# Cross attention on one core: turning the scores' rows in two row tiles, with a weighing put in front and every engine's order written anew

## The chip, the cores and the metric

One core of one Trainium2 chip runs the whole program. The metric is device time in microseconds; of several runs of a kernel the median is taken. The engines are TensorE (PE: matmuls and transposes, with its weight loads), VectorE (DVE), ScalarE (ACT), GpSimd (POOL) and SyncE (SP), whose queue issues the transfers.

## The reference

```python
x = x + tanh(g_xattn[0]) * cross(ctx, ctx, layernorm(x), mask, wq, bq, wk, bk, wv, bv, wo, bo)
x = x + tanh(g_ffn[0]) * switch(layernorm(x), Wq, Wk, Wv, Ws, Wd, Wo)

def cross(v, k, q, ...):                                  # x: (32, 112, 256), ctx: (32, 375, 256), 16 heads of 16
    qh, kh, vh = split(q @ wq + bq), split(k @ wk + bk), split(v @ wv + bv)
    logits = einsum('bhqd,bhkd->bhqk', qh, kh) / sqrt(16) + mask * -1e9
    attn = softmax(logits)
    return merge(einsum('bhqk,bhkd->bhqd', attn, vh)) @ wo + bo
```

The second layer (`switch`) is an attention over the 112 rows of x whose values and outputs are mixed from 8 experts chosen by a top 2 of gates. All is float32.

## The kernel before

The program has a short preparation, then a first half (`cross`, the first layer, all 32 batches) and a second half (`switch`, the second layer). The change is in `cross` alone.

**Groups and heads.** A batch has 16 heads in NG = 4 groups of G = 4. For each head PE computes the scores (`scores`, L439): 112 rows of queries by 375 keys, from three-part bfloat16 stacks (`Q_stack`, `K_stack`), into one of two banks. DVE adds the mask, copies the scores to `raw` and takes the row maximum (`score_max`, L759). POOL subtracts, giving `shifted` (`shift`, L876). When the four heads of a group are shifted, PE turns them (`turn`, L448): each head's 112 x 384 is turned in KC = 3 pieces of 128 keys, so 12 transposes a group, into the three banks of `bank_t`, one bank for each k. ACT takes the exponentials, one instruction a bank, into `probsT` (`exps`, L665). PE multiplies them with the values, weighing (`weigh`, L462): one matmul with 32 columns of weights for each k and head, into `bank_o` (the trace records 24 a group: each float32 one twice).

**Around them.** After the four groups ACT copies `headsT`, PE turns it back (`heads_back`, L470), DVE divides by the sums (`normalise`), PE turns (`heads_turn`, L477) and projects (`project`, L483), and DVE adds the result to x (`residual`). In the body of batch b PE also works ahead: for b + 2 the transposes of the context (`transposes`, L398), the keys in two halves (`keys`, L406), the turned x (`turn_x`, L414) and the queries (`queries`, L422), and for b + 1 the values (`values`, L430). Keys and queries are split into bfloat16 parts: keys by ACT, POOL (`key_rest`, L884) and DVE (`key_third`), queries by ACT (`query_copy`) and DVE (`split_queries`). They are stored to HBM and read back in stacked form (`exchange`, on SP's queue: L336, L338, L339, L344, L348).

**Order.** There is no scheduler. Every engine has a `body(b, ...)` that lists its work for one batch by hand, and runs it in that order; `batches` calls it for all 32, with the first two and the last two apart. Semaphores tie the engines: `turned`, `exp_done`, `pv_done`, `shift_done`, `scores_read` and so on, each counted through the batches. `shifted` and `probsT` have two buffers by the group's parity, `bank_t` one, so the turning of a group waits for the exponentials of the one before it, bank by bank. PE's order in a body of before is:

scores 0, 1; turning 3 of b - 1; score 2; transposes; score 3; weighing 3 of b - 1; score 4; keys 0; score 5; turning 0; scores 6, 7; keys 1; weighing 0; heads_back; score 8; turning 1; score 9; heads_turn; score 10; values 0, 1; score 11; weighing 1; score 12; project; score 13; turning 2; turn_x; scores 14, 15; values 2; queries; weighing 2.

The second half turns its scores in the manner that the change brings to the first: `HALVES` of 64 and 48 rows (L1169), then exponentials of ACT that write each half's columns (L1312).

Of the kernel before, what the change touches and what calls it, by code (L numbers as in the profile page):

```python
# [256 lines left out]
def cross(nc, z, d, c):  # L257
# [3 lines left out]
    VW = 32  # L261
    o = c.o
    with ExitStack() as ctx:
# [15 lines left out]
        probsT = sb("probsT", [KP, 2, KC, G * S])  # L279
# [32 lines left out]
        turned, exp_done, pv_done = sem("turned"), sem("exp_done"), sem("pv_done")  # L312
        headsT_copied, heads_ready, recip_done, heads_done = sem("headsT_copied"), sem("heads_ready"), sem("recip_done"), sem("heads_done")
# [73 lines left out]
        def _(pe):  # L387
# [123 lines left out]
            def body(b, p, i, first, ahead, last):  # L511
# [3 lines left out]
                S_ = lambda *hs: [scores(b, p, i, h, first) for h in hs]  # L515
                S_(0, 1)
                if back:
                    turn(b - 1, NG - 1, False)
                S_(2)
                if ahead:  # L520
                    transposes(b + 2, i + 1, p)
                S_(3)
                if back:
                    weigh(b - 1, 1 - p, NG - 1, False)
                S_(4)
                if ahead:
                    keys(b + 2, p, 0)
                S_(5)
                turn(b, 0, first)
                S_(6, 7)  # L530
                if ahead:
                    keys(b + 2, p, 1)
                weigh(b, p, 0, first)
# [7 lines left out]
                turn(b, 1, False)  # L541
                S_(9)
# [4 lines left out]
                S_(10)  # L547
                if front:
                    values(1 - p, 0)
                    values(1 - p, 1).then_inc(va_ready, 1)  # L550
                S_(11)
                weigh(b, p, 1, False)
                S_(12)
                if back:
                    project(b - 1)
                S_(13)
                turn(b, 2, False)
# [5 lines left out]
                S_(14, 15)  # L563
# [4 lines left out]
                if ahead:  # L568
                    queries(b + 2)
                elif front:  # L570
                    open_gates(b + 2 - B)
                weigh(b, p, 2, False)
# [37 lines left out]
            batches(pe, body)  # L610
            open_proj(0)
# [9 lines left out]
        def _(act):  # L621
# [57 lines left out]
            def body(b, p, i, first, ahead, last):  # L679
                second = isinstance(b, int) and b == 1  # L680
                if not first:
# [8 lines left out]
                if ahead:  # L690
# [7 lines left out]
                if ahead:  # L698
                    copy_x(b + 2)
                    query_copy(b + 2, p, i + 1)  # L700
                else:
                    e = b + 2 - B
                    act.wait_ge(o.xt_ready, e + 1)
                    act.activation(o.xnT[:, :, e, :], bank_ab[:, 0, 0:EC * S].rearrange("p (e s) -> p e s", e=EC), ACT.Copy).then_inc(o.xt_copied, 1)
                    if e == 0:
                        act.wait_ge(o.gates_ready, 1)
                        act.activation(o.gates[:, :, :].rearrange("s g e -> s (g e)"), bank_ab[0:S, 0, 0:2 * z.H2 * z.X], ACT.Copy).then_inc(o.gates_copied, 1)
# [35 lines left out]
        def _(dve):  # L743
# [65 lines left out]
            def body(b, p, i, first, ahead, last):  # L809
                second = isinstance(b, int) and b == 1  # L810
                if ahead:
# [3 lines left out]
                score_max(b, first, 0, 1)  # L815
                if not first and not last:
                    split_queries(b + 1)
                score_max(b, first, *range(2, 7))
# [7 lines left out]
                score_max(b, first, 8, 9, 10)  # L826
                if not last:
                    value_copy(b + 1, 1 - p, 0)
                score_max(b, first, 11, 12)
                if ahead:  # L830
                    key_third(b + 2, p)
                if not first:
                    residual(b - 1)
                score_max(b, first, 13, 14, 15)
                if not last:
                    value_copy(b + 1, 1 - p, 1)

# [31 lines left out]
        def _(pool):  # L869
            def shift(b, g, first):  # L870
# [693 lines left out]
```

## Time and profile before

| | us |
|---|---|
| median of 3 runs | 1300.96 |
| lowest and highest | 1298.34, 1303.64 |
| the profiled execution's own time | 1308.71 |
| its span, first to last instruction | 1307.0 |

The profile is of one execution. Its first half ends near 669 us of the span. A timeline row gives the start in us from the span's start, how long the merged instructions lasted from the first's start to the last's end, engine, line, operation, what it writes and reads, and how many there are. Pieces of PE overlap a little, since matmuls are pipelined.

### The profile page before, as it was taken

To read this page: it belongs to the slowest core of one execution; us is meant where nothing else is said; L and a number is where in the kernel's file an instruction comes from. 1 tells how busy PE (TensorE), PEld (TensorE's weight loads), DVE (VectorE), ACT (ScalarE), POOL (GpSimd) and SP (SyncE) were. 2 spreads that over 40 slices of the span, in tenths; PEclk is the share of its full clock that TensorE was granted. 3 is DMA by queue.
4 is the path that set the end of the run, shared out by engine and by line. 5 is a ranking of instruction groups with operands and counts; after the bars stand their busy time and mean duration, and the time that the engine had idled before them with its cause. 6 is when DMAs were issued, how large, how long until landed. Compare 5 with 4: busy or idle time off the path is not lost. (4 is left out here: it accounts for less than half of the span.)

```text
span 1307.0 us, 40360 instructions
## 1 busy us (share of the span) xinstructions
PE 1246.8 (95%) x15928; PEld 1017.5 (78%) x15928; DVE 866.8 (66%) x2455; ACT 611.9 (47%) x1353; POOL 550.3 (42%) x823
## 2 busy tenths in 40 slices
PE   5799999999999999999988999999999999999986
PEld 4577777787777777777667888888888888888874
DVE  2566766766766766766666667767766776676651
ACT  3455556556556556556434444334343443434331
POOL 3476676676676676666621122122122212221111
PEclk9999999999999999999999999999999999999997
DMA  8898897797787787786415666656666665666662
GB/s 224 192 196 190 191 199 170 165 189 159 161 184 159 158 185 157 161 185 146 103 43 116 151 137 137 155 133 141 142 149 131 139 161 132 141 143 150 144 133 77
DMA packets 262975, 200.21 MB, mean 153 GB/s; under 512 B 195906, under 2 KB 243844, under 8 KB 258692
## 3 DMA queue, kind: packets, MB, share of 16 engines
q1 hardware_dynamic: 262788, 197.64, 68.3%
q8 instruction: 127, 2.08, 0.7%
q14 instruction: 60, 0.49, 0.2%
HBM read 125.49 MB, written 72.11 MB: 151 GB/s over the span
## 5 line engine op out<-in xcount | busy, mean ns | idle before, releaser
L876 POOL TENSOR_SCALAR shifted<-raw,neg_max 112x375 f32<-112x375 f32 x512 | 304.5, 603 | 195.9 <-DVE neg_max L759 131.2
L759 DVE CUSTOM_DVE_ANT_0 raw<-bank_s,maskb 112x375 f32<-112x375 f32 x512 | 269.2, 545 | 119.5 <-issue 78.0
L665 ACT ACTIVATE probsT<-bank_t 128x448 f32<-128x448 f32 x384 | 181.0, 547 | 162.8 <-PE bank_t L448 162.8
L448 PE MATMUL bank_t<-ident,shifted 112*128 112x112 f32 x1536 | 170.3, 261 | 3.4 <-POOL shifted L876 3.4
L448 PEld LDWEIGHTS bank_t<-ident,shifted 112*128 112x128 f32 x1536 | 156.0, 141 | 22.3 <-POOL shifted L876 19.0
L439 PE MATMUL bank_s<-K_stack,Q_stack 128*112 128x375 bf16 x512 | 158.2, 337 | 13.5 <-DVE neg_max L759 8.1
L1467 POOL TENSOR_TENSOR mix_bd<-pm_te,tok 128x448 f32<-128x448 f32 x32 | 30.8, 963 | 232.8 <-DMA pm_te<-pm_dram 232.8
L1394 DVE TENSOR_REDUCE max<-bank_s 112x4 f32<-112x448 f32 x128 | 78.7, 615 | 74.8 <-PE bank_s L1157 74.8
L1109 PE MATMUL bank_ab<-xnT,wq2T 128*128 128x224 f32 x512 | 109.5, 357 | 0.8 <-ACT qT L1287 0.6
L1109 PE MATMUL bank_ab<-xnT,wk2T 128*128 128x224 f32 x512 | 109.7, 357 | 0.0
L1109 PEld LDWEIGHTS bank_ab<-xnT,wq2T 128*128 128x128 f32 x512 | 94.3, 190 | 11.6 <-issue 7.4
L1109 PEld LDWEIGHTS bank_ab<-xnT,wk2T 128*128 128x128 f32 x512 | 94.2, 190 | 10.2 <-issue 7.4
L462 PE MATMUL bank_o<-probsT,V 128*32 128x112 f32 x3072 | 101.2, 263 | 0.1
L462 PEld LDWEIGHTS bank_o<-probsT,V 128*32 128x32 f32 x3072 | 69.1, 109 | 39.4 <-issue 27.8
L439 PEld LDWEIGHTS bank_s<-K_stack,Q_stack 128*112 128x112 bf16 x512 | 62.7, 130 | 45.1 <-DVE neg_max L759 22.7
L203 POOL TENSOR_SCALAR var_eps<-moments 112x1 f32<-112x1 f32 x32 | 7.1, 223 | 213.5 <-DVE moments L199 213.4
L406 PE MATMUL bank_ab<-ctxT,wk_sb 128*128 128x375 f32 x256 | 93.1, 488 | 1.2 <-ACT ctxT L626 1.2
L430 PE MATMUL bank_ab<-wv_sb,ctxT 128*128 128x256 f32 x372 | 90.4, 379 | 0.0
L1397 DVE TENSOR_TENSOR shifted<-bank_s,max 112x448 f32<-112x448 f32 x128 | 79.9, 625 | 4.4
L430 PEld LDWEIGHTS bank_ab<-wv_sb,ctxT 128*128 128x128 f32 x372 | 68.8, 190 | 6.5
L1181 PEld LDWEIGHTS bank_g<-v,probsT 112*64 112x64 f32 (+1 forms) x1792 | 57.1, 130 | 19.7 <-issue 19.7
L1409 DVE COPY uT<-bank_g 128x448 f32<-128x448 f32 x32 | 20.0, 624 | 77.7 <-PE bank_g L1191 77.7
(144 smaller groups left out, 2250.7 us busy)
## 6 DMA issues: line engine op xcount, KB each, us to landing
K_stack<-k_dram SPq DMA_DIRECT2D x64, 562.5 KB, 7.5
k_dram<-k_parts SPq DMA_DIRECT2D x32, 562.5 KB, 5.1
att_dram<-att_q SPq DMA_DIRECT2D x32, 511.0 KB, 4.3
att_th<-att_dram SPq DMA_DIRECT2D x32, 511.0 KB, 5.3
v_dram<-mv SPq DMA_DIRECT2D x32, 455.0 KB, 7.2
v<-v_dram SPq DMA_DIRECT2D x32, 455.0 KB, 4.0
K_stack<-k_dram SPq DMA_DIRECT2D x32, 375.0 KB, 9.4
Q_stack<-q_dram SPq DMA_DIRECT2D x64, 168.0 KB, 9.2
```

The lines of the kernel that those rows point to most:

```text
L406: last = nc.tensor.matmul(bank_ab[:, t, 0:S2], c.wk[:, e, t * P:(t + 1) * P], ctxT[:, p, e, 0:S2], start=(e == 0), stop=(e == EC - 1))
L430: last = nc.tensor.matmul(dst, ctxT[:, p, e, k * KP:(k + 1) * KP], c.wv[:, e, :], start=(e == 0), stop=(e == EC - 1))
L439: nc.tensor.matmul(bank_s[h % 2][0:S, 0:S2], Q_stack[:, p, h, :], K_stack[:, p, h, :], start=True, stop=True).then_inc(scores_ready, 1)
L448: last = nc.tensor.transpose(bank_t[0:KP, k, j * S:(j + 1) * S], shifted[:, g % 2, j, k * KP:(k + 1) * KP], c.ident[0:S, 0:S])
L462: last = nc.tensor.matmul(bank_o[j * VW:(j + 1) * VW, g * S:(g + 1) * S], V[:, p, k, G * g + j, :], probsT[:, g % 2, k, j * S:(j + 1) * S] ...
L665: act.activation(probsT[:, g % 2, k, :], bank_t[0:KP, k, 0:G * S], ACT.Exp).then_inc(exp_done, 1)
L759: dve.tensor_tensor_reduce(raw[:, g % 2, j, :], bank_s[h % 2][0:S, 0:S2], c.maskb[:, :], -1.0, -LEAST, ALU.add, ALU.min, neg_max[:, g % 2, ...
L876: pool.tensor_scalar(shifted[:, g % 2, j, 0:S2], raw[:, g % 2, j, :], -1.0, neg_max[:, g % 2, j:j + 1], ALU.mult, ALU.add).then_inc(shift_ ...
L1109: last = nc.tensor.matmul(bank_ab[:, 0, m * 2 * S:(m + 1) * 2 * S], w, xnT[:, e, 2 * h:2 * h + 2, :].rearrange("p r s -> p (r s)"), start= ...
L1181: last = nc.tensor.matmul(weighed(half, m)[lo:hi, :], probsT[:, half, m, lo:hi], v[:, p, 2 * G * half + m, :], start=True, stop=True)
L1394: dve.tensor_reduce(neg_max[:, g % 2, :], sc, AXX, ALU.max).then_inc(max_done, 1)
L1397: dve.tensor_tensor(shifted[:, g % 2, :, :], sc, neg_max[:, g % 2, :].unsqueeze(2).to_broadcast([S, G, S]), ALU.subtract).then_inc(shift_d ...
```

## The change

`turn` splits the 112 rows of queries into `HALVES` of 64 and 48. A unit is one k and one head, u = 4k + j, twelve in a group. Each unit is turned by two transposes, one with rows 0 to 63 and one with rows 64 to 111 of the array. The lower half's units 0 to 7 go to bank 0 and the upper half's units 0 to 9 to bank 1; the rest share bank 2. The upper half runs with units 10 and 11 first, and the lower half's unit 8 waits for `upper_done`, so that both halves never write bank 2 at a time. `turned` is counted once a group instead of once a bank. `exps` has four instructions a group, one for each entry of `PLACES` (512, 480, 256 and 96 columns), which write the half's columns of each unit, and counts four. `turn` waits for all exponentials of the group before, and `weigh` for all of its own. `probsT` is indexed by unit.

PE's order becomes: transposes; scores 0, 1; weighing 2 of b - 1; turning 3 of b - 1; scores 2, 3; keys 0; score 4; weighing 3 of b - 1; scores 5, 6; keys 1; score 7; heads_back; score 8; turning 0; heads_turn; score 9; values 0, 1; score 10; weighing 0; turning 1; score 11; turn_x; score 12; project; score 13; queries; values 2; scores 14, 15; turning 2; weighing 1. ACT's, DVE's and POOL's orders follow. SP's queue is not touched.

```diff
+    UNITS, LOW = KC * G, z.S - 48
+    PLACES = ((0, 8, 0, 0, 0), (0, 10, 1, 1, 0), (8, 12, 0, 2, 0), (10, 12, 1, 2, 4 * LOW))
+    HALVES = ((0, LOW), (LOW, z.S))
...
-        probsT = sb("probsT", [KP, 2, KC, G * S])
+        probsT = sb("probsT", [KP, 2, UNITS, S])
...
             def turn(b, g, first):
                 pe.wait_ge(shift_done, H * b + G * g + G)
-                for k in range(KC):
-                    if not (first and g == 0):
-                        pe.wait_ge(exp_done, KC * (NG * b + g - 1) + k + 1)
-                    for j in range(G):
-                        last = nc.tensor.transpose(bank_t[0:KP, k, j * S:(j + 1) * S],
-                                                   shifted[:, g % 2, j, k * KP:(k + 1) * KP], c.ident[0:S, 0:S])
-                    last.then_inc(turned, 1)
+                if not (first and g == 0):
+                    pe.wait_ge(exp_done, len(PLACES) * (NG * b + g))
+
+                def one(half, u):
+                    lo, hi = HALVES[half]
+                    (bank, column), = [(bank, column + (u - first_u) * (hi - lo)) for first_u, end, h, bank, column in PLACES
+                                       if h == half and first_u <= u < end]
+                    k, j = u // G, u % G
+                    return nc.tensor.transpose(bank_t[0:KP, bank, column:column + hi - lo], shifted[lo:hi, g % 2, j, k * KP:(k + 1) * KP], c.ident[lo:hi, lo:hi])
+
+                for u in range(UNITS):
+                    if u == 8:
+                        pe.wait_ge(upper_done, NG * b + g + 1)
+                    one(0, u)
+                    last = one(1, (u + UNITS - 2) % UNITS)
+                    if u == 1:
+                        last.then_inc(upper_done, 1)
+                last.then_inc(turned, 1)
 
             def weigh(b, p, g, first):
...
+                pe.wait_ge(exp_done, len(PLACES) * (NG * b + g + 1))
                 for k in range(KC):
-                    pe.wait_ge(exp_done, KC * (NG * b + g) + k + 1)
                     for j in range(G):
                         last = nc.tensor.matmul(bank_o[j * VW:(j + 1) * VW, g * S:(g + 1) * S], V[:, p, k, G * g + j, :],
-                                                probsT[:, g % 2, k, j * S:(j + 1) * S], start=(k == 0), stop=(k == KC - 1))
+                                                probsT[:, g % 2, G * k + j, :], start=(k == 0), stop=(k == KC - 1))
...
             batches(pe, body)
+            weigh(B - 1, 1, NG - 2, False)
             open_proj(0)
             turn(B - 1, NG - 1, False)
             weigh(B - 1, 1, NG - 1, False)
...
             def exps(b, g, first):
                 if not (first and g < 2):
                     act.wait_ge(pv_done, NG * b + g - 1)
-                for k in range(KC):
-                    act.wait_ge(turned, KC * (NG * b + g) + k + 1)
-                    act.activation(probsT[:, g % 2, k, :], bank_t[0:KP, k, 0:G * S], ACT.Exp).then_inc(exp_done, 1)
+                act.wait_ge(turned, NG * b + g + 1)
+                for first_u, end, half, bank, column in PLACES:
+                    lo, hi = HALVES[half]
+                    act.activation(probsT[:, g % 2, first_u:end, lo:hi], bank_t[0:KP, bank, column:column + (end - first_u) * (hi - lo)].rearrange("p (u q) -> p u q", q=hi - lo),
+                                   ACT.Exp).then_inc(exp_done, 1)
...
             def body(b, p, i, first, ahead, last):
                 second = isinstance(b, int) and b == 1
+                if ahead:
+                    ctx_copy(b + 2, p, False)
                 if not first:
                     exps(b - 1, NG - 1, False)
                 if ahead:
-                    ctx_copy(b + 2, p, False)
+                    key_copy(b + 2, p, i + 1, 0)
                 if not first:
                     heads_copy(b - 1, second)
                 if ahead:
-                    key_copy(b + 2, p, i + 1, 0)
+                    key_copy(b + 2, p, i + 1, 1)
                 exps(b, 0, first)
-                if ahead:
-                    key_copy(b + 2, p, i + 1, 1)
-                exps(b, 1, first)
                 if not first:
                     out_copy(b - 1, second)
+                e = b + 2 - B
                 if ahead:
                     key_second(b + 2, p)
-                exps(b, 2, False)
-                if ahead:
                     copy_x(b + 2)
-                    query_copy(b + 2, p, i + 1)
                 else:
...
+                exps(b, 1, first)
+                if ahead:
+                    query_copy(b + 2, p, i + 1)
...
+                exps(b, 2, False)
```

On DVE `split_queries(b + 1)` moves to the front of the body, `moments_of` from the front to behind maximum 2, the first `value_copy` from behind maximum 10 to behind 9, `residual` stands behind maximum 12, `key_third` moves from behind maximum 12 to behind 13, and the second `value_copy` from the end to behind `key_third`. On POOL `key_rest` moves from behind shift 7 to before it.

## Rows read from the trace of the kernel before

**Rows 1.** The page, busy time by engine: us, share of the span, instructions.
```profile
PE 1246.8 (95%) x15928; PEld 1017.5 (78%) x15928; DVE 866.8 (66%) x2455; ACT 611.9 (47%) x1353; POOL 550.3 (42%) x823
```
**Rows 2.** Windows: us, busy time of each engine, PE's clock, DMA share, GB/s.
```profile
69.00:200.00 131.00, 129.73 (x1397) 104.30 (x1395) 91.78 (x306) 74.74 (x162) 88.88 (x134) 1.00 0.89 194
...
340.00:640.00 300.00, 294.25 (x3168) 235.09 (x3167) 208.72 (x693) 168.90 (x365) 202.30 (x308) 1.00 0.77 167
...
415.50:430.40 14.90, 14.90 (x143) 11.81 (x145) 10.09 (x35) 7.49 (x17) 11.58 (x18) 1.00 0.99 218
```
**Rows 3.** Who waited for whom, 69 to 625 us: us in total, times, longest.
```profile
PE bank_s L439 <- DVE neg_max L759: 6.3, 28, 0.6
```
**Rows 4.** Timeline of PE, 400 to 421 us.
```profile
400.84 0.65 PE L470 MATMUL bank_ab<-ident,headsT 128*112 128x128 f32 x4
...
401.49 1.32 PE L448 MATMUL bank_t<-ident,shifted 112*128 112x112 f32 x12
402.64 0.33 PE L439 MATMUL bank_s<-K_stack,Q_stack 128*112 128x375 bf16 x1
...
404.88 0.32 PE L439 MATMUL bank_s<-K_stack,Q_stack 128*112 128x375 bf16 x1
405.13 0.78 PE L462 MATMUL bank_o<-probsT,V 128*32 128x112 f32 x24
405.85 0.37 PE L439 MATMUL bank_s<-K_stack,Q_stack 128*112 128x375 bf16 x1
...
411.51 0.53 PE L439 MATMUL bank_s<-K_stack,Q_stack 128*112 128x375 bf16 x2
...
414.10 0.78 PE L462 MATMUL bank_o<-probsT,V 128*32 128x112 f32 x24
415.09 0.37 PE L439 MATMUL bank_s<-K_stack,Q_stack 128*112 128x375 bf16 x1 [0.21 <-DVE neg_max L759]
...
420.26 0.65 PE L470 MATMUL bank_ab<-ident,headsT 128*112 128x128 f32 x4
```
**Rows 5.** Timeline of the second half, 1004.6 to 1005.6 us.
```profile
1004.65 0.66 PE L1169 MATMUL bank_t<-ident,shifted 64*112 64x64 f32 x16
...
1005.13 0.71 PE L1157 MATMUL bank_s<-kT,qT 64*112 64x112 f32 x10
1005.35 0.60 ACT L1312 ACTIVATE probsT<-bank_t 112x512 f32<-112x512 f32 x1
```
**Rows 6.** Groups by line, 340 to 640 us: busy us, mean ns of one.
```profile
L759 DVE CUSTOM_DVE_ANT_0 raw<-bank_s,maskb 112x375 f32<-112x375 f32 x247 | 129.9, 545 | 53.7 <-issue 37.4 <-PE bank_s L439 14.2
L665 ACT ACTIVATE probsT<-bank_t 128x448 f32<-128x448 f32 x186 | 87.7, 547 | 77.4 <-PE bank_t L448 77.4
L884 POOL TENSOR_TENSOR k<-k,k_parts 128x750 f32<-128x750 f32 x15 | 23.5, 1563 | 4.7 <-ACT k_parts L636 4.6
L677 ACT ACTIVATE outT<-bank_ab 128x224 f32<-128x224 f32 x16 | 6.0, 378 | 0.0
```
**Rows 7.** Timeline of SP's queue, 411 to 432 us.
```profile
414.60 0.38 SPq L338 DMA_DIRECT2D q_dram<-q_parts  x1
...
415.67 1.40 SPq L344 DMA_DIRECT2D K_stack<-k_dram  x3
417.68 1.37 SPq L348 DMA_DIRECT2D Q_stack<-q_dram  x3
```
**Rows 8.** DMA issues, 340 to 640 us, last row 69 to 200 us: median us to landing.
```profile
k_dram<-k_parts SPq DMA_DIRECT2D x15, 562.5 KB, 5.0
...
Q_stack<-q_dram SPq DMA_DIRECT2D x16, 112.0 KB, 9.9
...
k_dram<-k_parts SPq DMA_DIRECT2D x7, 562.5 KB, 6.8
```
**Rows 9.** Timeline of the last group, 655 to 690 us.
```profile
661.35 1.32 PE L448 MATMUL bank_t<-ident,shifted 112*128 112x112 f32 x12
...
661.99 1.42 ACT L665 ACTIVATE probsT<-bank_t 128x448 f32<-128x448 f32 x3 [2.62 <-PE bank_t L448]
```

More of the change, by code:

```diff
@@ L312, in cross @@
         turned, exp_done, pv_done = sem("turned"), sem("exp_done"), sem("pv_done")
+        upper_done = sem("upper_done")
         headsT_copied, heads_ready, recip_done, heads_done = sem("headsT_copied"), sem("heads_ready"), sem("recip_done"), sem("heads_done")
@@ L515, in body @@
                 S_ = lambda *hs: [scores(b, p, i, h, first) for h in hs]
+                if ahead:
+                    transposes(b + 2, i + 1, p)
                 S_(0, 1)
                 if back:
+                    weigh(b - 1, 1 - p, NG - 2, False)
                     turn(b - 1, NG - 1, False)
-                S_(2)
+                S_(2, 3)
                 if ahead:
-                    transposes(b + 2, i + 1, p)
-                S_(3)
+                    keys(b + 2, p, 0)
+                S_(4)
                 if back:
                     weigh(b - 1, 1 - p, NG - 1, False)
-                S_(4)
-                if ahead:
[L527 to L530, printed above, removed]
+                S_(5, 6)
                 if ahead:
                     keys(b + 2, p, 1)
-                weigh(b, p, 0, first)
+                S_(7)
                 if last:
@@ L540, in body @@
                 S_(8)
-                turn(b, 1, False)
-                S_(9)
+                turn(b, 0, first)
                 if ahead:
@@ L546, in body @@
                     heads_turn(b - 1)
-                S_(10)
+                S_(9)
                 if front:
@@ L550, in body @@
                     values(1 - p, 1).then_inc(va_ready, 1)
+                S_(10)
+                weigh(b, p, 0, first)
+                turn(b, 1, False)
                 S_(11)
[L552 to L557, printed above, removed]
                 if ahead:
@@ L562, in body @@
                     open_x(b + 2 - B)
-                S_(14, 15)
+                S_(12)
+                if back:
+                    project(b - 1)
+                S_(13)
+                if ahead:
+                    queries(b + 2)
+                elif front:
+                    open_gates(b + 2 - B)
                 if front:
@@ L567, in body @@
                     values(1 - p, 2).then_inc(vb_ready, 1)
-                if ahead:
[L569 to L572, printed above, removed]
+                S_(14, 15)
+                turn(b, 2, False)
+                weigh(b, p, 1, False)
             def turn_weights(*numbers):
@@ L680, in body @@
                 second = isinstance(b, int) and b == 1
+                if ahead:
+                    ctx_copy(b + 2, p, False)
                 if not first:
@@ L810, in body @@
                 second = isinstance(b, int) and b == 1
+                if not first and not last:
+                    split_queries(b + 1)
+                score_max(b, first, 0, 1, 2)
                 if ahead:
@@ L814, in body @@
                     o.moments_of(dve, c.X[0:S, b + 2 - B, :], b + 2 - B)
[L815 to L818, printed above, removed]
+                score_max(b, first, 3, 4, 5, 6)
                 if ahead:
@@ L825, in body @@
                     normalise(b - 1, second)
-                score_max(b, first, 8, 9, 10)
+                score_max(b, first, 8, 9)
                 if not last:
                     value_copy(b + 1, 1 - p, 0)
-                score_max(b, first, 11, 12)
+                score_max(b, first, 10, 11, 12)
+                if not first:
+                    residual(b - 1)
+                score_max(b, first, 13)
                 if ahead:
                     key_third(b + 2, p)
-                if not first:
-                    residual(b - 1)
-                score_max(b, first, 13, 14, 15)
                 if not last:
                     value_copy(b + 1, 1 - p, 1)
+                score_max(b, first, 14, 15)
             def copy_weights(*numbers):
@@ L869, in _, with shift @@
         def _(pool):
-            def shift(b, g, first):
-                for j in range(G):
+            def shift(b, g, first, members=range(G)):
+                for j in members:
                     h = G * g + j
-                    free = [] if j or (first and g < 2) else [(turned, KC * (NG * b + g - 1))]
+                    free = [] if j or (first and g < 2) else [(turned, NG * b + g - 1)]
                     wait_all(pool, v_set, (scores_read, H * b + h + 1), *free)
@@ L903, in body @@
                     o.inverse_deviation(pool, b + 2 - B)
-                shift(b, 1, first)
+                shift(b, 1, first, range(G - 1))
                 if ahead:
                     key_rest(b + 2, p)
+                shift(b, 1, first, (G - 1,))
                 shift(b, 2, first)
```

10 lines of the change are left out of this document (4 added, 6 removed).

## The prediction

> **What bounds the kernel now.** First the busy shares [rows 1]: TensorE (PE) is busy 95% of the span. The shares mix two halves, so the windows come next [rows 2]: in 340 to 640 us, the middle of the first half, PE is busy 294.25 of 300 us at clock 1.00, VectorE (DVE) 208.72, ScalarE (ACT) 168.90, GpSimd (POOL) 202.30, DMA 0.77. DMA stands at 0.89 before 200 us, where x is still being loaded. Then who waited for whom, 69 to 625 us [rows 3]: PE's longest wait, scores for the row maximum, is 6.3 us in all. So the first half is PE's instruction stream, and the last view is that stream [rows 4]: the same piece (L470) starts at 400.84 and 420.26, a batch of 19.42 us, and I find one stall in it, where the score at 415.09 follows a weighing that began at 414.10 and elsewhere hands over after 0.71 to 0.72 (405.13 to 405.85): 0.28 us.
>
> The reader is to see how PE pieces hand over. A piece is drawn until its last result is out. The next begins 0.16 to 0.17 us before that end when it uses the array in the same shape (401.49+1.32=402.81, next at 402.64), but only 0.07 us before it when the shape changes: the score at 404.88 ends at 405.20, the weighing (128 rows by 32 columns) begins at 405.13. A change therefore costs about 0.09 us, and a score is followed after 0.16 us by a turning but after 0.25 us by a weighing [rows 4].
>
> **The turning in two row tiles.** Before, a group's turning is 12 whole transposes, 1.15 us from its start to the next piece's (401.49 to 402.64), 0.096 us each [rows 4]. No row has the split one with 128 columns, but the second half turns 64 and 48 rows with 112 columns [rows 5]: from the start of 16 halves to the next piece, of the same shape, are 0.48 us. If the first pair takes 0.10, as a whole one does, the other seven take 0.055 each. Drawn, the 16 halves last 0.66 us; twelve pairs will be 0.66+4x0.055 = 0.88 us, and as the next piece has another shape it begins 0.07 before that end: 0.81 us. The bounds for the wider weights: nothing more, or all in proportion, 0.055x128/112 = 0.063 us a pair, which is +0.10 us a group. I take nothing, since with whole transposes 0.096 us holds a load of 128 columns too and did not wait for it longer than for 112 moving ones; the other end is kept. The wait inside the turning, before unit 8, is for a matmul started six pairs, 0.33 us, earlier whose result is out 0.66-0.48+0.04 = 0.22 later: nothing, at worst 0.05.
> Sum: 4x(1.15-0.81) = -1.36 us a batch.
> The Trainium skill, TensorEngine Tiling (Array Packing), section Instruction Overhead, gives each matmul some 60 cycles beside its columns, so that narrow ones save little. By it at 2.4 GHz (the granted 1.00) a whole transpose is (112+60)/2.4 = 72 ns and a half of 64 columns 52 ns, an estimate of 20 ns saved a unit where the rows give 41: over 48 units and 29 batches 29 us less than my sum, some 1293. The rows have 96 ns for the whole one, so the trace does not agree with it there.
>
> **Changes of shape.** Before: four weighings a batch entered at +0.09 (their way out is in the 0.71). After: turnings 0 and 2 follow a score or ordinary piece, +0.18; turnings 1 and 3 stand right behind a weighing, whose way out is paid anyway, 0; the weighing of group 1 follows turning 2, whose way out is in the 0.81, so one entry less, -0.09. Net +0.09. Without "another group in front" this would be +0.36.
>
> **Order on PE.** The same pieces otherwise. More scores now stand before another score or the keys (0.20 us: two drawn as 0.53, one as 0.33) than before a transpose (0.16): +0.07 over the order. The stall of 0.28 goes if score 4 no longer follows score 2 so closely: weighing and keys lie between. PE's sum: 19.42-1.36+0.09+0.07-0.28 = 17.94 us.
>
> **Do the others keep up at 17.94?** I wrote the new orders as a timetable from the rows' durations, t in us from score 0. PE's steps are read from the 31 pieces between 400.84 and 420.26, of which [rows 4] has the first and last: keys 1.26, values 1.72 and 0.86, project 0.86, queries 0.97, heads_back 0.49, transposes 0.65, heads_turn and turn_x 0.19, weighing 0.71. Then scores 0, 1 start at 0 and 0.20; weighing 2 0.46; turning 3 1.17; scores 2, 3 1.98, 2.19; keys 2.39; score 4 3.65; weighing 3 3.90; scores 5, 6 4.61, 4.82; keys 5.02; score 7 6.28; heads_back 6.44; score 8 6.93; turning 0 7.18; heads_turn 8.00; score 9 8.20; values 8.36; score 10 10.08; weighing 0 10.33; turning 1 11.05; score 11 11.86; turn_x 12.02; score 12 12.21; project 12.42; score 13 13.28; queries 13.48; values 14.45; scores 14, 15 15.32, 15.52; turning 2 15.78; weighing 1 16.59; transposes 17.30; the next score 0 17.95.
>  Per batch ACT has 11 us of work, DVE 13.5, POOL 13.1 (shares of [rows 2] by 19.42), ACT's to grow by 0.2: no engine becomes the bound. ACT: exps are now four of 512, 480, 256 and 96 columns. A 512 one with this very output pattern takes 0.60 [rows 5]; 448 take 0.547 and 224 take 0.378 [rows 6], so 0.57, 0.40 and 0.28 for the rest. Three of 0.547 are drawn as 1.42 [rows 9], so each starts 0.12 before the end of the one ahead: 1.48 us for all four. None can begin until the whole turning is out, 0.10 behind it, say ([rows 5] has 0.04, 1005.31 to 1005.35): they end 0.88+0.10+1.48 = 2.46 after it began, where before they ended 663.41-661.35 = 2.06 after. The rest of ACT's queue behind them (keys, headsT) has idle time. What is late next:
>
> turning 2 at 15.8 ends 16.7, exps end 18.2, weighing 2 stands at 17.94+0.46 = 18.4: slack 0.1;
> turning 3 at 1.2, exps end 3.6, weighing 3 at 3.9: slack 0.2;
> turning 0 at 7.2, exps 9.6, weighing 0 at 10.3: 0.6; group 1 over 2.
> score 6 at 4.8 needs maximum 4 (score 4 at 3.65, read 0.46 later, 0.55 on DVE [rows 6]): slack 0.1; heads_turn behind turning 0 at 8.0 needs heads from 7.5: none.
> POOL: the key rest (1.56 us [rows 6]) is put before shift 7; that shift ends 9.7 and turning 1 waits for it at 11.0. Turnings come later than before against the scores, but shifts of group 2 need only turning 0 (8.0; shift 8 at 9.7).
> I charge 0.1 us a batch for these tight places.
> Costed at nothing: the split of queries put first on DVE (the queries are copied by 15.6, so the split ends 0.6, maximum 0 by 1.0, and its bank is wanted at 1.98), x's moments, add of bias, and the moved values: each has a gap of over 0.3 us behind it in that timetable.
>
> **DMA.** Before, the transfers of a batch run as one burst: busy 0.99 from 415.5 to 430.4, idle in the 4 us before [rows 2]. It starts when the queries are split (first q_dram issue 414.60, 3.1 us after score 0 at 411.51), K_stack 415.67, the last Q_stack issue 418.6 plus 9.9 to land = 428.5 [rows 7, 8], 2.4 us before the next score 0 (411.51+19.42 = 430.9). After, the split is ready at 0.6 instead of 3.1, but the keys' store (issued 15.5, 5.0 to land) must have landed too: 20.5-17.94 = 2.6 into the batch. K_stack then goes at 2.6 and all is in by 2.6+12.8 = 15.4 to 16: 2 us of slack, as before. In the batches that also load x, DMA is busy 0.89x19.42 = 17.3 of the new 17.94 us [rows 2], and the store takes 6.8 rather than 5.0 us [rows 8]: K_stack at 4.4, in by 17.2, with no room for a longer burst. I charge 0.5 us a batch over six: 3 us; the bounds are 0 and 1 us each.
>
> **Sum.** Batches 1 to 29 have the full order: 29x(1.48-0.1) = 40.0; early DMA +3. Batch 0 lacks turning 3 and saves perhaps 0.7; batches 30 and 31 hold no keys and wait for the maxima anyway: 0. At the end nothing hides the exps, so the last group's 2.46 against 2.06 us [rows 9] is +0.4, and weighing 2, which now stands 1.52 after the start of turning 2 (0.81+0.71), waits for its exps about 1.0. Total -40.0+3-0.7+1.4 = -36.3 us. The profiled execution took 1308.71 us (span 1307.0) and would take 1272.4; the runs' median, 1300.96, is 7.75 lower, and I carry that difference over: 1264.7, say **1265 us**.
>
> **Rivals.**
> The chain through the exps binds in part (weighings 2 and 3 at slack 0.1 and 0.2, DVE's maximum likewise). Each 0.1 us more of wait in two groups is 0.2x29 = 6 us. With 0.2 to 0.5 us more a group, or pairs at 0.063 us as well (4x0.10x29 = 12 us), 1273 to 1290. For it: slacks are thin. Against: the same way of writing out the old order gives 19.44 for the 19.42 measured.
> The halves take turns in the array instead of running side by side: a pair then costs 0.055+0.042 = 0.097 us, 4x11x0.042 = 1.85 us a batch more than I take, which eats 1.48: +0.37x29 = 11 us, **1312**. It decides from 0.089 us a pair on. Against: 16 halves in 0.66 us [rows 5].
> The split saves half as much, a pair at 0.076 us, halfway between 0.055 and the 0.097 above: 4x11x0.021x29 = 27 us of the gain go, **1291**. For it: a 128-column load in a row tile is in no row. Against: the same loads fit in 0.096 us with 112 moving columns. The Trainium skill's fixed cost per matmul, cited above, would come out near this.
> Nothing comes of it: the bound moves to DMA and the burst follows period for period. That wants over 19.3 us of transfers a batch; the rows show 15 (17.3 early). Time 1298 to 1304.
> Also possible: no tight place binds and early DMA hides: 3+3 us less, 1259.
>
> **How the numbers follow.** The measurement can tell 0.5%, 6.5 us. My forecast, 1256 to 1273, the 1259 in it: 0.62. Partly bound, 1273 to 1290: 0.22. Half the saving, about 1291: 0.03. Below 1256: 0.04. No change: 0.04. Slower: 0.05, 0.03 of it the halves taking turns, 0.02 the exps' chain longer by over 0.8 us a group. The range goes from 1254 (3 us of scatter of the runs below 1257, the bare 1.48 in 29 batches) to 1283, the middle of the partly bound case: some 0.2 lie outside. Faster 0.91, same 0.04, slower 0.05.
>
> **What would show it.** In the profile after: a group's 24 half transposes drawn as 0.88 us; the piece behind at +0.81; scores of one place 17.95 to 18.1 apart from 200 to 600 us; four exps of 0.60, 0.57, 0.40, 0.28. Wrong would be: weighings waiting for ACT over 0.2 us, K_stack landing behind score 0, a pair above 0.063 us, PE's clock under 1.00 in the first half, or a period that stays over 18.6.

## The result and the profile after

Medians of four runs each on one chip: 1300.49 us before, 1264.70 us after (1261.05 to 1267.14). The ratio is 0.972, with an interval of 0.9696 to 0.9743. The forecast was 1265 us. The profiled execution took 1262.39 us, its span is 1260.7.

The windows of the kernel after, as in [rows 2]: us, busy time of each engine (PE, PE's loads, DVE, ACT, POOL), clock, DMA share, GB/s.
```profile
69.00:200.00 131.00, 130.89 (x1821) 100.71 (x1820) 100.06 (x328) 82.18 (x204) 96.64 (x147) 1.00 0.94 203
340.00:600.00 260.00, 257.75 (x3623) 197.69 (x3624) 197.16 (x646) 159.85 (x395) 189.63 (x289) 1.00 0.81 178
```
PE is still the bound: 257.75 of 260 us, at clock 1.00. The transfers are denser, 0.81 for 0.77, and 0.94 for 0.89 where x is loaded.

PE's timeline of one batch after, the answer to [rows 4]:
```profile
405.11 0.96 PE L460 MATMUL bank_t<-ident,shifted 64*128 64x64 f32 x24
406.00 0.78 PE L482 MATMUL bank_o<-probsT,V 128*32 128x112 f32 x24
406.71 0.87 PE L406 MATMUL bank_ab<-ident,ctx_in 128*128 128x128 f32 x6
407.42 0.48 PE L447 MATMUL bank_s<-K_stack,Q_stack 128*112 128x375 bf16 x2
407.84 0.78 PE L482 MATMUL bank_o<-probsT,V 128*32 128x112 f32 x24
408.55 0.95 PE L460 MATMUL bank_t<-ident,shifted 64*128 64x64 f32 x24
409.44 0.53 PE L447 MATMUL bank_s<-K_stack,Q_stack 128*112 128x375 bf16 x2
...
414.50 0.96 PE L460 MATMUL bank_t<-ident,shifted 64*128 64x64 f32 x24
415.46 0.38 PE L497 MATMUL bank_ab<-ident,heads 112*128 112x112 f32 x2
...
418.54 0.95 PE L460 MATMUL bank_t<-ident,shifted 64*128 64x64 f32 x24
419.42 0.37 PE L447 MATMUL bank_s<-K_stack,Q_stack 128*112 128x375 bf16 x1
...
423.17 0.96 PE L460 MATMUL bank_t<-ident,shifted 64*128 64x64 f32 x24
```
Turning 2 starts at 405.11 and again at 423.17: a batch of 18.06 us for 19.42 [rows 4]. A turning is drawn as 0.95 to 0.96 us and hands over after 0.89 (408.55 to 409.44), where it was 1.15. Only at 415.46 does the next piece start when the turning is out, not 0.07 us before: heads_turn waits for the heads, which DVE finishes at 415.31.

ACT's timeline of the same batch after, and the exps by size (the groups of 340 to 600 us), for [rows 6]:
```profile
406.18 1.48 ACT L686 ACTIVATE probsT<-bank_t 128x512 f32<-128x512 f32 x4 [1.13 <-PE bank_t L460]
...
409.61 1.48 ACT L686 ACTIVATE probsT<-bank_t 128x512 f32<-128x512 f32 x4 [1.18 <-PE bank_t L460]
```
```profile
L686 ACT ACTIVATE probsT<-bank_t 128x512 f32<-128x512 f32 x57 | 34.0, 596 | 45.2 <-PE bank_t L460 45.2
L686 ACT ACTIVATE probsT<-bank_t 128x480 f32<-128x480 f32 x57 | 32.4, 569 | 0.0
L686 ACT ACTIVATE probsT<-bank_t 128x256 f32<-128x256 f32 x57 | 22.5, 395 | 0.0
```
The exps begin 0.11 us behind the turning's end (405.11+0.96 = 406.07) and last 1.48 us. Those of group 2 are done at 407.66, and weighing 2 starts at 407.84: 0.18 us to spare.

SP's queue after, for [rows 7], and landings in 340 to 600 us, for [rows 8]:
```profile
404.86 0.38 SPq L344 DMA_DIRECT2D k_dram<-k_parts  x1
407.83 0.38 SPq L346 DMA_DIRECT2D q_dram<-q_parts  x1
...
409.67 1.38 SPq L352 DMA_DIRECT2D K_stack<-k_dram  x3
```
```profile
k_dram<-k_parts SPq DMA_DIRECT2D x14, 562.5 KB, 4.4
...
Q_stack<-q_dram SPq DMA_DIRECT2D x15, 112.0 KB, 10.0
```
The queries' store goes 0.4 us after score 0 (407.42) instead of 3.1, K_stack 2.25 us after it. Over the batches of the full order the stacks land 2.2 to 4.7 us before they are wanted.

The end of the first half after, for [rows 9]:
```profile
622.71 0.78 PE L482 MATMUL bank_o<-probsT,V 128*32 128x112 f32 x24 [0.93 <-ACT probsT L686]
623.42 1.97 PE L528 MATMUL bank_s<-wv2T,xnT 128*112 128x512 f32 x4
625.32 0.96 PE L460 MATMUL bank_t<-ident,shifted 64*128 64x64 f32 x24
628.21 0.78 PE L482 MATMUL bank_o<-probsT,V 128*32 128x112 f32 x24 [1.93 <-ACT probsT L686]
```
Weighing 2 waits 0.93 us for its exps and weighing 3 waits 1.93.

Where the time went, by the two traces: from the first score of batch 0 to that of batch 31, 602.2 us before and 560.8 after, -41.4; from there to the second half's first queries 25.7 and 29.7, +4.1. Together -37.3 us. Two pieces changed sides of these cuts. The transposes of batch 2 now stand before the first score, where they take 1.3 us (43.73 to 45.04), and weighing 2 of batch 30 stands behind the first score of batch 31 (0.7 us). Like for like the batches gave -39.4 us, the end +3.3, and the change -36.0.

The start took 2.4 us more (the first score at 45.0 for 42.6), 1.3 of it these transposes. The second half, whose code is the same, took 625.0 for 636.5 us. Of these 11.5 us, 7.6 lie in its last 60 us or so. There the granted clock stood at half (1.2 GHz) for 23.9 us before and for 10.3 us after; the same eight matmuls (`wo2T`, `uT`) last 3.6 to 3.7 us at that level and 1.95 at the full one. Another 2.8 us lie in its first 45 us; whether the first half's new end has a part in them is not shown. In the twelve other profiles of this study it takes 627 to 637 us, so the 625.0 is a short one. The profiled executions differ by 46 us and the medians by 36.

### The profile page after: what moved, and what is told of

It is laid out like the page before. It is cut to its first block and busy times, and to the rows that moved or that the text cites. A ratio compares the mean times of both kernels' runs of the same rounds, so it can differ in the third digit from the quotient of the medians.

```text
span 1260.7 us, 43560 instructions
## 1 busy us (share of the span) xinstructions
PE 1208.4 (96%) x17464; PEld 967.8 (77%) x17464; DVE 869.2 (69%) x2455; ACT 619.6 (49%) x1481; POOL 550.5 (44%) x823
## 5 line engine op out<-in xcount | busy, mean ns | idle before, releaser
L899 POOL TENSOR_SCALAR shifted<-raw,neg_max 112x375 f32<-112x375 f32 x512 | 326.0, 645 | 164.4 <-DVE neg_max L781 120.6
L781 DVE CUSTOM_DVE_ANT_0 raw<-bank_s,maskb 112x375 f32<-112x375 f32 x512 | 266.5, 544 | 102.8 <-issue 87.7
L686 ACT ACTIVATE probsT<-bank_t 128x512 f32<-128x512 f32 (+3 forms) x512 | 189.2, 459 | 104.2 <-PE bank_t L460 104.2
L447 PE MATMUL bank_s<-K_stack,Q_stack 128*112 128x375 bf16 x512 | 151.2, 336 | 4.9 <-DVE neg_max L781 4.6
L460 PEld LDWEIGHTS bank_t<-ident,shifted 64*128 64x128 f32 (+1 forms) x3072 | 105.3, 139 | 27.8 <-issue 24.5
L460 PE MATMUL bank_t<-ident,shifted 48*128 48x48 f32 (+1 forms) x3072 | 122.6, 226 | 0.0
L1133 PEld LDWEIGHTS bank_ab<-xnT,wk2T 128*128 128x128 f32 x512 | 94.1, 190 | 10.3 <-issue 7.4
L1311 ACT ACTIVATE qT<-bank_ab 128x448 f32<-128x448 f32 x64 | 34.8, 543 | 72.9 <-PE bank_ab L1133 72.9
```

The costliest lines, as they stand in the source:

```text
L447: nc.tensor.matmul(bank_s[h % 2][0:S, 0:S2], Q_stack[:, p, h, :], K_stack[:, p, h, :], start=True, stop=True).then_inc(scores_ready, 1)
L460: return nc.tensor.transpose(bank_t[0:KP, bank, column:column + hi - lo], shifted[lo:hi, g % 2, j, k * KP:(k + 1) * KP], c.ident[lo:hi, lo ...
L686: act.activation(probsT[:, g % 2, first_u:end, lo:hi], bank_t[0:KP, bank, column:column + (end - first_u) * (hi - lo)].rearrange("p (u q) ...
L781: dve.tensor_tensor_reduce(raw[:, g % 2, j, :], bank_s[h % 2][0:S, 0:S2], c.maskb[:, :], -1.0, -LEAST, ALU.add, ALU.min, neg_max[:, g % 2, ...
L899: pool.tensor_scalar(shifted[:, g % 2, j, 0:S2], raw[:, g % 2, j, :], -1.0, neg_max[:, g % 2, j:j + 1], ALU.mult, ALU.add).then_inc(shift_ ...
L1133: last = nc.tensor.matmul(bank_ab[:, 0, m * 2 * S:(m + 1) * 2 * S], w, xnT[:, e, 2 * h:2 * h + 2, :].rearrange("p r s -> p (r s)"), start= ...
```

## The experiments

A batch's time below is the median distance of two first scores, from each run's trace.

**Order alone, tiles alone.** `order_only` is the kernel before with the bodies of all engines as after (and weighing 2 in front of the end); `tiles_only` is the kernel after with the bodies of before. Short diffs against before and after:
```diff
 # order_only, against before
+                if ahead:
+                    transposes(b + 2, i + 1, p)
                 S_(0, 1)
                 if back:
+                    weigh(b - 1, 1 - p, NG - 2, False)
                     turn(b - 1, NG - 1, False)
...
 # tiles_only, against after
-                if ahead:
-                    transposes(b + 2, i + 1, p)
                 S_(0, 1)
-                if back:
-                    weigh(b - 1, 1 - p, NG - 2, False)
-                    turn(b - 1, NG - 1, False)
-                S_(2, 3)
+                if back:
+                    turn(b - 1, NG - 1, False)
+                S_(2)
+                if ahead:
+                    transposes(b + 2, i + 1, p)
+                S_(3)
...
```


> The new orders of all engines with the whole transposes and the three exps a group of before. Theory (PE's steps add up): a batch of 18.07 us plus 4 x 0.264 for whole turnings (1.151 for 0.887), less 0.18 for the entries of turnings 0 and 2, plus 0.09 for weighing 1 behind turning 2: 19.04 us, 0.37 under before, so some 1290 us. Rival (the order is what pays, by taking away waits): under 18.5 us a batch, 1275 or less. Rival (the order alone is worth nothing): 19.4 us, 1300.

> The turning in two row tiles and the four exps, in the orders of before. Theory: 19.42 - 1.06 + 4 x 0.09 for four entries into the row tiles = 18.72 us of PE's own work, and weighing 3 comes 1.96 us after the start of turning 3 but its exps end 2.5 after: a wait of 0.5 us, which may swallow the 0.28 of score 4. 19.0 to 19.3 us a batch, 1288 to 1297. Rival (exps are covered in the old order too): 18.7 to 18.8, 1281.

Measured: `order_only` 1286.02 us, ratio 0.9882 (0.9849 to 0.9916), 18.95 us a batch. `tiles_only` 1318.85 us, ratio 1.0126 (1.0102 to 1.0149), 19.71 us a batch. The first is 0.09 us under the sum of PE's steps (19.04); 0.28 us of its gain of 0.47 is the stall of score 4, whose weighing hands over after 0.71 there. The second is slower than before and beyond my expectation (19.0 to 19.3 us). PE's timeline of `tiles_only`:
```profile
414.08 1.03 PE L438 MATMUL bank_ab<-wv_sb,ctxT 128*128 128x256 f32 x4
415.13 1.15 PE L430 MATMUL bank_ab<-xnT,wq_sb 128*128 128x112 f32 x8
416.20 0.78 PE L482 MATMUL bank_o<-probsT,V 128*32 128x112 f32 x24
416.92 0.53 PE L447 MATMUL bank_s<-K_stack,Q_stack 128*112 128x375 bf16 x2
417.37 0.95 PE L460 MATMUL bank_t<-ident,shifted 64*128 64x64 f32 x24
...
419.12 0.32 PE L447 MATMUL bank_s<-K_stack,Q_stack 128*112 128x375 bf16 x1
419.97 0.78 PE L482 MATMUL bank_o<-probsT,V 128*32 128x112 f32 x24 [0.53 <-ACT probsT L686]
```
Weighing 3 (419.97) stands 0.85 us behind a score that hands over in 0.25: 0.60 us for the exps, as expected (0.5). What I had left out is, first, at 415.13: the values before the queries hand over after 1.05 us, and the queries take 1.07 to the next piece, where both were 0.86 and 0.97. On ACT the copy of the turned x stood behind four exps that now begin after the whole turning.

**One instruction moved in `tiles_only`.**
```diff
-                exps(b, 2, False)
                 if ahead:
                     copy_x(b + 2)
+                exps(b, 2, False)
+                if ahead:
                     query_copy(b + 2, p, i + 1)
```


> As tiles_only (19.71 us a batch), but ACT copies the turned x before the exps of group 2. Theory (the four exps hold up what stands behind them on ACT, which PE's queries wait for, 0.19+0.10 us a batch): the queries no longer wait, weighing 2 is late enough for the later exps: 19.42 us a batch, some 1310 us. The wait of weighing 3 for its exps stays at 0.6 us. Rival (only the wait at weighing 3 and the shapes cost): 19.7.

Measured: 1312.90 us, ratio 1.0045 (1.0023 to 1.0067), 19.42 us a batch. In its timeline the queries follow the values after 0.86 us again, and weighing 3 still waits:
```profile
408.76 0.82 PE L447 MATMUL bank_s<-K_stack,Q_stack 128*112 128x375 bf16 x2
409.42 1.03 PE L438 MATMUL bank_ab<-wv_sb,ctxT 128*128 128x256 f32 x4
410.28 1.04 PE L430 MATMUL bank_ab<-xnT,wq_sb 128*128 128x112 f32 x8
...
415.02 0.78 PE L482 MATMUL bank_o<-probsT,V 128*32 128x112 f32 x24 [0.52 <-ACT probsT L686]
```
The two scores of 408.76 also hand over late: score 14 after 0.46 us for 0.24 in the kernel before, as the weights of score 15 wait for DVE's maximum of score 13. So the old order's balance can be written out, by the same batch in both traces. The four turnings are 1.10 us shorter. Going into them and coming out of them costs 0.51 us (0.33 on the way in, 0.18 on the way out; I had set 0.36 in all). Weighing 3 waits 0.60, less the stall of 0.28 that is gone. Score 15 costs 0.22 and weighing 0, which waits for its exps, 0.08. That is 1.13 us against 1.10, and `tiles_only` loses 0.29 more at the queries.

**Changes of shape.** `apart` puts a score between a weighing and the turning next to it, in three places:
```diff
-                weigh(b, p, 0, first)
-                turn(b, 1, False)
-                S_(11)
+                weigh(b, p, 0, first)
+                S_(11)
+                turn(b, 1, False)
...
-                S_(14, 15)
-                turn(b, 2, False)
+                S_(14)
+                turn(b, 2, False)
+                S_(15)
                 weigh(b, p, 1, False)
```
and likewise score 1 between weighing 2 and turning 3.

> The kernel after, with one score moved between weighing 2 and turning 3, between weighing 0 and turning 1, and between turning 2 and weighing 1. Theory: three changes of shape more at 0.09 us each, less up to 0.04 for each score that no longer stands beside another: 0.15 to 0.27 us a batch more, 1269 to 1273. Rival (a change of shape costs nothing when an engine order around it is free): 18.07 us, 1265.

Measured: 1280.63 us, ratio 0.9827 (0.9793 to 0.9862), 18.49 us a batch, +0.42 for the three. More than the 0.15 to 0.27 expected. Its timeline:
```profile
414.78 0.32 PE L447 MATMUL bank_s<-K_stack,Q_stack 128*112 128x375 bf16 x1
415.04 0.96 PE L460 MATMUL bank_t<-ident,shifted 64*128 64x64 f32 x24
415.92 0.37 PE L447 MATMUL bank_s<-K_stack,Q_stack 128*112 128x375 bf16 x1
416.22 0.78 PE L482 MATMUL bank_o<-probsT,V 128*32 128x112 f32 x24
```
A score behind a piece of its own shape hands over to another shape after 0.26 us (414.78 to 415.04). One that is itself the first after a change lasts 0.37 for 0.32 and hands over after 0.30 (415.92 to 416.22). Against the 0.16 of a score amid its own shape a lone score between two changes costs 0.14 us, and three make the 0.42.

**Does the chain through the exps bind?** `five_exps`:
```diff
-    PLACES = ((0, 8, 0, 0, 0), (0, 10, 1, 1, 0),
+    PLACES = ((0, 4, 0, 0, 0), (4, 8, 0, 0, 4 * LOW), (0, 10, 1, 1, 0),
```


> The kernel after, with the exp of 512 columns as two of 256: the chain from turning to weighing is 0.16 us longer in every group. Theory (PE bound, slack of 0.18 and 0.22 us at weighings 2 and 3): 18.07 to 18.12 us a batch, 1265 to 1267. Rival (the chain through the exps binds): 0.16 us in two to four groups, 18.4 to 18.7, 1274 to 1283.

Measured: 1267.45 us, ratio 0.9734 (0.9709 to 0.9759), 18.07 us a batch. But the chain is not 0.16 us longer:
```profile
405.89 1.54 ACT L686 ACTIVATE probsT<-bank_t 128x256 f32<-128x256 f32 x5 [1.14 <-PE bank_t L460]
```
The five exps are drawn as 1.54 us for the 1.48 of four, since the second 256 columns start 0.28 us behind the first. The slack falls from 0.18 to 0.12 us at weighing 2 and from 0.22 to 0.16 at weighing 3. The chain does not bind, in this kernel or in the kernel after, but only 0.06 us more of it was put to the test; that 0.16 us would be covered is not shown.

**What spaces the pairs.** The turning came out at 0.89 us for the 0.81 of the sum. In the trace the two halves of a pair start within 20 ns of each other, so it is the pairs that are spaced. `load96`, `load124` and `load120` load and turn fewer of the 128 columns from batch 1 on (the rest of each piece is left out and keeps old values):
```diff
+                    wide = KP if b == 0 else 96
-                    return nc.tensor.transpose(bank_t[0:KP, bank, column:column + hi - lo], shifted[lo:hi, g % 2, j, k * KP:(k + 1) * KP], c.ident[lo:hi, lo:hi])
+                    return nc.tensor.transpose(bank_t[0:wide, bank, column:column + hi - lo], shifted[lo:hi, g % 2, j, k * KP:k * KP + wide], c.ident[lo:hi, lo:hi])
```


> The kernel after, but from batch 1 on each half transpose loads and turns 96 of the 128 columns; the last 32 of each piece are left out and keep older values. Theory (the weight load sets the spacing): a pair every 0.049 us, (96 columns by the line through 0.055 at 112 and 0.062 at 128), 4 x 11 x 0.013 = 0.6 us a batch less. Rival (the moving side has a floor, and 0.055 was it): a pair every 0.055 us, 0.3 us a batch less. Rival (neither, the wider piece was spaced by the rows of the group): 0.062.

> As load96 with 120 columns, the last 8 left out. Theory (load of 0.0623 x 120/128 = 0.058 above the floor of 0.055): a pair every 0.058 us, whatever the rule on multiples up to 8. Rival (multiples of 16): 0.10 or more.

> As load96 with 124 of 128 columns loaded and turned from batch 1 on, the last 4 left out. moved125 had a pair of half transposes every 0.109 us with 125 columns, load96 every 0.055 with 96. Theory (an odd number of columns is what makes a load slow): a pair every 0.060 us, between 0.055 and 0.062. Rival (only multiples of 16 are fast): 0.105 to 0.109.

The weight loads of the turning by width, one row of each kernel, 340 to 600 us (mean ns of one stands before the second bar). `load96`:
```profile
L461 PEld LDWEIGHTS bank_t<-ident,shifted 64*96 64x96 f32 x696 | 42.2, 123 | 12.3 <-issue 11.0 <-POOL shifted L900 1.3
```
`load120`:
```profile
L461 PEld LDWEIGHTS bank_t<-ident,shifted 64*120 64x120 f32 x696 | 44.6, 134 | 12.3 <-issue 11.0 <-POOL shifted L900 1.3
```
`load124`:
```profile
L461 PEld LDWEIGHTS bank_t<-ident,shifted 64*124 64x124 f32 x684 | 45.7, 137 | 12.2 <-issue 10.8 <-POOL shifted L900 1.3
```
`moved125`, below, with the row of its values:
```profile
L460 PEld LDWEIGHTS bank_t<-ident,shifted 64*125 64x125 f32 x612 | 70.4, 185 | 10.9 <-issue 10.6 <-POOL shifted L899 0.2
...
L438 PEld LDWEIGHTS bank_ab<-wv_sb,ctxT 128*125 128x125 f32 x153 | 26.7, 188 | 2.9
```
The kernel after:
```profile
L460 PEld LDWEIGHTS bank_t<-ident,shifted 64*128 64x128 f32 x690 | 47.3, 139 | 12.3 <-issue 11.0 <-POOL shifted L899 1.3
```
Measured (median distance of successive 64-row matmuls of a turning, and a batch): 96 columns 0.056 us and 17.81; 120 columns 0.058 and 17.91; 124 columns 0.060 and 18.01; 128 columns 0.062 and 18.07. With 112 columns the second half has 0.055 to 0.056. From 96 to 112 the spacing does not move, so something other than the load is the floor there; what it is, no run varies. Above it the spacing follows the width. That it is the load and not the width of the output, which changes with it, is the reading that fits the load's own durations (123, 134, 137 and 139 ns); no run parts the two. One run of each took 1266.97, 1274.37 and 1274.94 us; the batches above say more.

**Trying to better it.** `moved` sets score 9 before heads_turn, and at the end of the first half lets the open_proj pieces cover the two waits for exps. `moved125` and `moved126` also turn three pieces of 125 (exactly 375) or 126 columns, in `shifted`, `probsT` and `V`.
```diff
                 turn(b, 0, first)
+                S_(9)
                 if ahead:
                     pe.wait_ge(k_copied, 2 * EC * (b + 3))
                 if back:
                     heads_turn(b - 1)
-                S_(9)
...
-            weigh(B - 1, 1, NG - 2, False)
             open_proj(0)
+            weigh(B - 1, 1, NG - 2, False)
             turn(B - 1, NG - 1, False)
+            open_proj(1)
             weigh(B - 1, 1, NG - 1, False)
...
 # moved126
-        SK = KC * KP
+        SK, W = KC * KP, 126
```


> The kernel after, unchanged, beside the two that try to better it. Both theories: 1261 to 1268 us, 18.07 us a batch.

> The kernel after with score 9 before heads_turn, and at the end of the first half open_proj(0) ahead of weighing 2 and open_proj(1) ahead of weighing 3. Theory: heads_turn stalls 0.07 us for the heads and that goes, and the neighbours are cheaper by 0.02: 17.98 us a batch, 2.6 us in all; the end of the first half waits 0.9 and 1.9 us for exps, and some 1.6 of it goes: 4 us less than the kernel after. Rival (another wait takes their place): 0 to 1 us less.

> As moved, and 375 keys turned as three pieces of 125 columns for three of 128 with padding. Theory (a pair of half transposes is spaced by its weight load, 0.055 us at 112 columns and 0.062 at 128): 48 pairs at about 0.0610 for 0.0623, 0.06 us a batch, 1.8 us less than moved. Rival (the spacing steps by something else than the columns): 0.

> As moved, with pieces of 126 columns, an even number, instead of 128 (three hold the 375 keys and 3 of padding). Theory (the load spaces the pairs, 0.060 us at 124 and 0.062 at 128, and only an odd number is slow): 0.061 us a pair, 18.03 - 4 x 11 x 0.001 = 17.98 us a batch, 1.5 us less than moved, 3 to 5 less than the kernel after. Rival (only multiples of 4 are fast): a pair at 0.1 us or more, over 19.5 us a batch.

Measured: `after_again` 1272.76 us, ratio 0.9737 (0.9710 to 0.9763); `moved` 1270.72, 0.9729 (0.9703 to 0.9754), 18.03 us a batch; `moved125` 1343.30, 1.0292 (1.0263 to 1.0321), 20.26 us; `moved126` 1269.13, 0.9712 (0.9680 to 0.9745), 18.00 us. The small gains a batch are there in the traces, 0.04 and 0.03 us; in the time they cannot be told from nothing. The end takes 28.8 us for the 29.7 of the kernel after, less than the 1.6 us hoped for. In `after_again`, the same kernel as after, it took 31.4. There the granted clock fell to half (1.2 GHz) for 3.4 us from 630.8 on, behind three waits of PE of 0.92, 1.92 and 0.76 us, and four matmuls that take 1.88 us in the profile of after took 3.30:
```profile
629.07 0.78 PE L482 MATMUL bank_o<-probsT,V 128*32 128x112 f32 x24 [1.92 <-ACT probsT L686]
...
631.34 3.30 PE L528 MATMUL bank_s<-wv2T,xnT 128*112 128x512 f32 x4
```
A stretch of half clock, 3.4 to 6.8 us long, stands at this end in 10 of the 12 kernels with the row tiles that were profiled, and in neither of the two with whole transposes. So the waits at the end can cost clock besides their own time, and what `moved` gives back lies between 0.9 us (beside after) and 2.6 (beside `after_again`).

`moved125` fails for one reason:
```profile
412.27 1.52 PE L460 MATMUL bank_t<-ident,shifted 64*125 64x64 f32 x24
413.72 0.53 PE L447 MATMUL bank_s<-K_stack,Q_stack 128*112 128x375 bf16 x2
```
A turning takes 1.45 us instead of 0.89: a pair every 0.109 us, for 0.060 with 124 columns. Four of these 0.56 us are the 2.23 us a batch by which it is slower than `moved`.

## Why the prediction was right, point by point

**PE's stream is the bound, and its steps add up: shown.** The table of starts, t from score 0 at 407.42, met the trace within 0.2 us: weighing 2 at 0.46 and measured at 0.42, turning 3 at 1.17 and 1.13, turning 0 at 7.18 and 7.08, score 12 at 12.21 and 12.40. `order_only` came out at 18.95 where the same sum said 19.04. `tiles_only` shows where the sum ends: it had 19.0 to 19.3 and missed 19.71, as waits of PE came in that I had not written out.

**The turning, 0.81 us: a term mis-sized.** It is 0.89, four times 0.075, so 0.30 us a batch. I took the weight load's width to cost nothing and kept the proportional 0.063 us a pair as the other end; the truth, 0.062, is at that end. The ground I gave, that a load of 128 columns fits in the 0.096 us of a whole transpose, is no evidence for 0.055. The width probes show a floor of 0.055 and the load above it.

**The remaining pieces, 0.2 us too dear.** It was made up by what I had carried over unchanged: the queries in front of the values hand over after 0.88 us (421.00 to 421.88) for 0.97, as they no longer stand before a change of shape; heads_back after 0.44 for 0.49; a score before the keys after 0.16 for 0.20. The transposes went the other way, 0.71 for 0.65, as the first piece after a weighing. So 17.94 and the 0.1 for tight places met 18.07 through two errors that cancel: luck, in part.

**Changes of shape: right in kind, a little low.** 0.09 us for an entry holds where the piece ahead is in a row of its own shape. `apart` shows that a lone one costs 0.14, and `tiles_x_first` that coming out of a turning costs another 0.04 to 0.06, which my sum holds only in part.

**The stall of score 4: gone**, as said. Score 4 starts 3.64 us into the batch, 3.65 in the table.

**The exps: right.** 0.596, 0.569 and 0.395 us for 0.60, 0.57 and 0.40, 1.48 for all four; slack at weighing 2 0.18 us for 0.1. From the turning's start to the last exp it is 2.55 us (405.11 to 407.66) for 2.46, as the turning is drawn as 0.96 us for 0.88. The rival in which they bind in part falls with this slack, and `five_exps` agrees. Only heads_turn of the tight places waits, 0.07 us a batch.

**DMA: no charge.** I set 3 us for the batches that load x. That term was not needed. They have the same 18.06 to 18.07 us as the others but for one of 18.40; the transfers close up to 0.94 and the stacks still land at least 2.2 us early.

**The end: mis-sized.** Like for like +3.3 us, for +1.4. Weighing 3 waits 1.93 us, since the last turning's exps end 2.84 us after it began, for 2.46. Another 2.2 of the 3.3 us lie before the last turning, where weighings 2 and 3 of batch 30 and 0 and 2 of batch 31 wait 0.5, 0.2, 0.8 and 0.9 us for exps that have nothing beside them; I had only the last of these.

**The sum: right by terms that cancel.** Like for like, batches 1 to 29 gave -38.9 us for -37.0 with the DMA charge (-40.0 without it). Batch 30, which I set at 0, gave -1.3. Batch 0 cost 0.9 where I expected 0.7 less: its clock stood at half until 50.8 us, before only until 46.1. With the end this makes -36.0 for -36.3. The mechanism held, but that the total is so near is luck.

**The carry to the median.** I carried over 7.75 us between the profiled execution of before and its median. The second half alone differed by 11.5 us between the two profiles, most of it in its tail under more or less half clock, so such a gap says little of the kernel. The predicted profiled execution, 1272.4, missed the 1262.4 by 10 us; that the median met 1264.7 owes something to luck.

**The halves do run side by side**, and the rival on the slower side falls: 24 halves in 0.96 us, the two of a pair starting within 20 ns. A pair at 0.062 us is also under the 0.076 of the rival that saves half. What I had not listed as a rival is how the slower side is in fact reached: the same turning in the old order, 1.3% slower. The order alone is worth 0.47 us a batch, the tiles alone cost 0.29, both together give 1.35.

## What to carry to other kernels

Write PE's pieces out with how each hands over to its neighbour, shape changes included: on an engine without gaps that sum met the batch within 0.13 us, and it prices a new order before it is built, as long as no wait comes in that it does not hold. Making a piece shorter by merging its signals lengthens the chain behind it; look at every instruction that stands behind the longer one in its engine's queue, or the gain goes where `tiles_only` lost it. Put pieces of other shapes next to one another, and never a single ordinary one between two of them.

## What the runs showed of the hardware

Pairs of half transposes are 0.055 to 0.056 us apart with 96 or 112 columns of weights, then 0.058, 0.060 and 0.062 with 120, 124 and 128 (0.062 with 126 too). With 125 columns the transpose's float32 load lasts 185 ns instead of 137 and the pairs are 0.109 us apart; with 126 it lasts 138 ns. The float32 loads of ordinary matmuls take about that long at every width that the traces hold: 190 ns with 128 columns, 188 with 126 and with 125, 176 with 112. So at 125 a transpose loses the shorter load that it has at 124, 126 and 128, while the values, whose weights have the same 125 columns, lose nothing. One odd width was run, so that it is oddness is the reading that fits, not a rule shown. The score that is first after a change of shape lasts 0.37 us, 0.05 more than one amid its own.
